# Keys stacked by DMA and the second attention taken batch by batch, in a two-layer decoder kernel

## The reference, cut to what matters

```python
# experts of layer 0: each token sums its 4 experts' rows, then a layer norm -> x
routed = zeros_like(x).at[tok].add(out_slots * flat_w[order][:, None])
# attention of layer 1, masked
q = einsum('bsh,he->bse', x, w_q)          # 16 heads x 128
k, v = split(einsum('bsh,he->bse', x, w_kv), 2)   # 4 groups x 128 each
probs = softmax(q @ k.T * 128 ** -0.5); ctx = probs @ v; out = ctx @ w_dense
# recurrence: query x, keys and values the context
log_D = ...; D = exp(log_D - max_log_D)     # 128 x 384 causal cells per head
qk = einsum('bhsd,bhtd->bhst', qh, kh) / sqrt(dh)
C = qk * D; h = (C / normalizer) @ vh; out = layernorm_per_head(h)
```

## Time and profile before

| | us |
|---|---|
| median of 3 runs | 1097.9 (1096.1 to 1100.84) |
| profiled execution, its own time | 1096.5 |
| its span, first to last instruction | 1094.5 |
| TensorE busy in it | 999.0 (91%) |
| VectorE, ScalarE, GpSimd busy | 717.9, 608.3, 459.8 |
| mean granted TensorE clock | 0.958 |

### The profile page before, as it was taken

The page is one execution under the profiler, slowest core; times in us unless marked ns, Lnnn a source line. Parts: engine busy times, 40 slices in busy tenths (PEclk is TensorE's granted clock), DMA queues, the critical chain, the costliest instruction groups (busy, mean ns, idle before and its releaser), DMA issues. The chain is left out here.

```text
span 1094.5 us, 18969 instructions
## 1 busy us (share of the span) xinstructions
PE 999.0 (91%) x6064; PEld 815.0 (74%) x6064; DVE 717.9 (66%) x2146; ACT 608.3 (56%) x1654; POOL 459.8 (42%) x473
## 2 busy tenths in 40 slices
PE   7999999998996799669899999988878889999996
PEld 5998899887883689537678888965445568777775
DVE  5666766663588456446655767646787557888886
ACT  3656565656222455336576776547874556555553
POOL 5787667761287344366111110210137214444321
PEclk9999999999998899869899999989998989999998
DMA  6732111000011799624301101001003011112101
GB/s 207 257 124 79 30 31 29 16 15 2 1 63 52 253 345 338 212 73 140 95 20 60 33 25 40 1 22 52 2 2 116 1 58 58 58 58 67 50 1 39
DMA packets 83784, 85.61 MB, mean 78 GB/s; under 512 B 8577, under 2 KB 75975, under 8 KB 83568
## 3 DMA queue, kind: packets, MB, share of 16 engines
q1 hardware_dynamic: 79776, 75.59, 21.4%
q0 software_dynamic: 3072, 7.34, 2.2%
q10 hardware_dynamic: 848, 1.57, 0.4%
HBM read 63.36 MB, written 22.02 MB: 78 GB/s over the span
## 5 line engine op out<-in xcount | busy, mean ns | idle before, releaser
L579 POOL TENSOR_TENSOR a_qk<-h,a_by_sin 128x512 f32<-128x512 f32 x64 | 81.9, 1280 | 5.0
L352 DVE CUSTOM_DVE_ANT_0 h<-a_score_ps,mask_bf 128x128 f32<-128x128 f32 (+1 forms) x128 | 40.7, 355 | 64.5 <-PE a_score_ps L345 64.3
L1286 POOL TENSOR_TENSOR a_w_l<-a_w,a_w_h 128x256 fp32r<-128x256 f32 x30 | 21.8, 728 | 115.6 <-ACT a_w_h L1479 115.4
L358 ACT ACTIVATE y_moe<-y_moe,a_nmax 128x128 f32<-128x128 f32 x64 | 25.6, 400 | 75.9 <-DVE a_nmax L352 75.9
L339 DVE COPY a_probsT<-a_turn_ps 128x384 f32<-128x384 f32 x64 | 34.9, 546 | 48.2 <-PE a_turn_ps L269 48.2
L1025 POOL TENSOR_TENSOR e_w_l<-e_w,e_w_h 128x512 fp32r<-128x512 f32 x32 | 40.8, 1276 | 53.1 <-ACT e_w_h L1093 53.1
L80 PE MATMUL a_proj_ps<-a_x_l,a_w_h 128*128 128x512 f32 x128 | 57.2, 447 | 3.6 <-POOL a_w_l L584 3.4
L459 PEld LDWEIGHTS a_proj_ps<-a_w,xT 128*128 128x128 f32 x512 | 59.6, 192 | 0.9 <-issue 0.2
L459 PE MATMUL a_proj_ps<-a_w,xT 128*128 128x128 f32 x512 | 59.8, 275 | 0.0
L755 PE MATMUL t_y_ps<-wo,attnT 128*128 128x256 f32 x256 | 58.7, 383 | 0.0
L2629 POOL TENSOR_TENSOR m_up_l<-m_up_w,m_up_h 128x1024 fp32r<-128x1024 f32 x8 | 19.5, 2434 | 90.1 <-ACT m_up_h L2601 90.1
(11 more groups left out here) (464 smaller groups left out, 3516.2 us busy)
## 6 DMA issues: line engine op xcount, KB each, us to landing
slots<-zeros SPq DMA_DIRECT2D x4, 2048.0 KB, 8.0
e_rows<-slots SPq DMA_DIRECT2D x32, 256.0 KB, 4.7
e_w<-in_L_ffn_w_dram SPq DMA_DIRECT2D x32, 256.0 KB, 4.9
out_slots<-e_out SPq DMA_DIRECT2D x32, 256.0 KB, 4.2
e_w<-in_L_ffn_w_dram SPq DMA_DIRECT2D x32, 128.0 KB, 4.3
a_w<-in_L_attn_w_q_dram SPq DMA_DIRECT2D x32, 128.0 KB, 2.2
m_up_w<-in_up_dram SPq DMA_DIRECT2D x8, 512.0 KB, 3.7
a_w<-in_L_attn_Wq_dram SPq DMA_DIRECT2D x16, 128.0 KB, 2.3
```

The lines of the kernel that those rows point to most:

```text
L352: done = dve.tensor_tensor_reduce(self.probs[:, b, cells], self.score_ps[:, r, cells], self.k.mask_bf[:, cells], -1.0, 3e38, ALU.add, ALU. ...
L358: act.activation(self.probs[:, b, 0:P], self.probs[:, b, 0:P], ACT.Exp, bias=self.nmax[:, b, 0:1], scale=-1.0, accum_out=self.total[:, b, ...
L579: pool.tensor_tensor(qk[:, par, 0 if what == "q" else 1, half * HALF:(half + 1) * HALF], by_cos[:, r, :], by_sin[:, r2, :], ALU.add).then_ ...
```

## The change

Second attention: units go batch by batch, over all heads of a batch. A step now makes two heads' queries for one batch (256 tokens), from a weight tile of 128x512, with 12 matmuls of 256 columns; there are still 32 steps. Keys are made per batch and group. Keys and values are kept for two batches, and `q` and the weight tiles get places of their own. Each gather has its own semaphore, and VectorE adds a row as soon as it has landed. Two tiles are prepared per batch, during the batch before.

Keys of the recurrence: SyncE stores the context's two parts to DRAM during the projection (4 stores of 512 KB) and loads them back in stacked form, 8 loads of 256 KB for each half, the first half during the projection, the second at the start of the recurrence. The `spread` constant is halved. The gates block then makes only the 16 stacks of x.

Around it: the block with two loads is gone; the twelve small loads are issued half by SyncE, half by GpSimd, and TensorE waits per batch instead of SyncE for all; two of the mixture's loads move into the recurrence; `C` gets its own memory.

```diff
-    STEPS = 2 * H
+    PAIRS = H // 2
+    STEPS = B * PAIRS
...
-                 ("x", 2)]
...
+        first = [("x", 0), ("v", 0), ("x", 1), ("v", 1), ("k", (0, 0)), ("q", 0), ("k", (1, 0))]
...
+            step = u // 2
+            return step, 2 * (step % PAIRS) + u % 2, step // PAIRS
...
+                gather(0)
+                gather(1)
+                ln.power(pool, 0)
+                ln.power(pool, 1)
+                gather(2)
+                for b in range(1, B):
+                    step, t = PAIRS * (b - 1), QT * b
+                    cut_low(step + 2)
+                    if b == 1:
+                        gather(t + 1, early)
+                    cut_low(step + 3)
+                    ln.power(pool, t)
+                    if b == 1:
+                        gather(t + 1, late)
+                    cut_low(step + 4)
...
+                        for a in range(2):
+                            for c in range(DC):
+                                last = product(pe, out[:, a * S:(a + 1) * S], weights(which, c, a),
+                                               x_p[:, c, b * S:(b + 1) * S], c == 0, c == DC - 1)
...
-                    dve.wait_ge(fetched[t], TOP0 * 16)
                     for j in range(TOP0 - 1):
+                        dve.wait_ge(fetched[t][j], 16)
...
+            @block.sync            # projection
+            def _(sp):
+                for c in range(DC):
+                    for part, (done, rows) in enumerate(((c_high, k.c_p.h), (c_low, k.c_p.l))):
+                        sp.wait_ge(done, c + 1)
+                        sp.dma_start(k.key_parts[part * D + c * P:part * D + (c + 1) * P, :], rows[:, c, :].bitcast(F32)
+                                     ).then_inc(k.keys_stored, 16)
+                sp.wait_ge(projected, 1)
+                sp.wait_ge(wo_low, WO_CUTS)
+                sp.wait_ge(k.keys_stored, 16 * 2 * DC)
+                load_keys(sp, k, 0)
...
+def load_keys(sp, k, half):
+    for part in range(2):
+        source = k.key_parts[part * D:(part + 1) * D, half * HALF:(half + 1) * HALF].rearrange("(c i w) t -> i w c t", i=2, w=LW)
+        for i in range(2):
+            for again in range(2):
+                first = i * 4 * LW + part * 2 * LW + again * LW
+                sp.dma_start(k.keys[half][first:first + LW, :, :].bitcast(F32), source[i]).then_inc(k.keys_in[half], 16)
...
-                for n in range(4 * STACKS):
+                for n in range(2 * STACKS):                       # stacks in the gates block
...
+            @block.gpsimd          # gates
+                pool.wait_ge(nM_done, 1)
+                spread_rows(pool, 1)
+                spread_rows(pool, 3)
...
-                sp.wait_ge(k.nM_in, 16 * B * 3)
+                spread_rows(sp, 0)
+                spread_rows(sp, 2)
...
+                    if h == 0:                                     # recurrence
+                        pe.wait_ge(k.nM_in[b], 16 * 3)
...
-        layer1_lstm_load(nc, k, I)
```

More of the change, by code:

```diff
@@ L1247, in of, with keys, value @@
         def of(u):
[L1249 to L1256, removed]
+            step = u // 2
+            return step, 2 * (step % PAIRS) + u % 2, step // PAIRS
+        def keys(b, i, j):
+            return slice(b % KEPT * S + i, b % KEPT * S + j)
+        def value(t):
+            return t % (KEPT * QT)
         with nc.Block() as block:
@@ L1290, in _ @@
                 ln.power(pool, 0)
+                ln.power(pool, 1)
                 gather(2)
[L1292 to L1312, removed]
+                for b in range(1, B):
+                    step, t = PAIRS * (b - 1), QT * b
+                    early, late = (0, 1), (2, 3)
+                    cut_low(step + 2)
[6 more added lines that the diff above has]
+                    cut_low(step + 4)
+                    cut_low(step + 5)
+                    ln.power(pool, t + 1)
+                    cut_low(step + 6)
+                    if b + 1 < B:
+                        gather(t + 2, early)
+                    cut_low(step + 7)
+                    if b + 1 < B:
+                        gather(t + 2, late)
+                    cut_low(step + 8)
+                    if b + 1 < B:
+                        gather(t + 3, early)
+                    cut_low(step + 9)
+                    if b + 1 < B:
+                        gather(t + 3, late)
+                for step in range(STEPS - PAIRS + 2, STEPS):
                     cut_low(step)
@@ L1363, in mix @@
                     g = head // HPG
-                    at.mix(pe, u, u % 4, lambda j: v[:, 2 * b + j, g * HD:(g + 1) * HD])
+                    at.mix(pe, u, u % 4, lambda j: v[:, value(QT * b + j), g * HD:(g + 1) * HD])
                 for one in first:
@@ L1487, in _ @@
                 keep("v", 0)
-                keep("x", 1)
-                keep("v", 1)
-                ln.squares(act, 2)
-                for one in first[-4:]:
+                for one in first[2:]:
                     keep(*one)
-                ln.squares(act, 3)
+                cut_high(2)
                 for u in range(UNITS):
@@ L1675, in layer1_gates @@
         nM, left, left2 = (m.sb(f"g_{n}", [P, CAUSAL]) for n in ("nM", "left", "left2"))
-        parts = m.sb("g_parts", [P, 3, CAUSAL], BF16)
+        parts = k.nM_parts
         x_p = Parts(m, "g_x", [P, DC, T])
         st_ps = m.ps("g_st_ps", [P, 4, 512])
-        BY_DVE = [n for n in range(4 * STACKS) if n >= 12 and n % 2]
-        BY_ACT = [n for n in range(4 * STACKS) if n not in BY_DVE]
+        BY_DVE = [11, 13, 15]
+        BY_ACT = [n for n in range(2 * STACKS) if n not in BY_DVE]
         x_high, x_low = m.sem("g_x_high"), m.sem("g_x_low")
@@ L1798, in _, with spread_rows @@
                 dve.wait_ge(kept, 1)
+            def spread_rows(queue, b):
+                for i in range(3):
+                    queue.dma_start(k.nM_rows[i * ROWS:i * ROWS + LH, b, :], parts[b * ROWS:b * ROWS + LH, i, :]
+                                    ).then_inc(k.nM_in[b], 16)
             @block.gpsimd
```

194 lines of the change are left out of this document (88 added, 106 removed).

## The result

| | before | after |
|---|---|---|
| median, us | 1097.12 (1096.1 to 1100.84, 4 runs) | 1086.26 (1081.75 to 1087.43, 4 runs) |
| ratio, 95% interval | | 0.9889 (0.9862 to 0.9916) |
| profiled execution; its span | 1096.5; 1094.5 | 1087.43; 1085.1 |
| mean granted clock | 0.958 | 0.960 |

The change takes 1.1% off by the ratio, 10.9 us by the medians. So most of this part asks which terms were too small, and whether errors hide each other. They do.

A forecast was written before the change was run, and what follows sets the result against it. TensorE, busy 91% of the span, was taken as the bound. Terms: -5.1 - 1.0 - 1.1 - 1.5 + 1.4 + 0.4 = -6.9 us, from the median 1097.9 to 1091.0 us; range 1082 to 1098.

The forecast's parts named there:

- Gates block: Gates block without key stacks: ends at 745.4, held by GpSimd's six loads at 1.1 us each; gain 5.1 us.
- The lower bound: Gates block: GpSimd's six small loads at SyncE's 0.63 us each end at 742.5, behind VectorE; gain 7.5 us.
- The block with two loads: Between projection and gates: one border and two issues go; gain 1.0 us.
- The keys: Recurrence's keys by DMA: loads land by 731, by the 256 KB row (4.7 us), needed at about 746; zero cost.
- The serial bound: Key loads, the other end: eight one after the other at 4.7 us each take 37.6 us, landing at 752.
- The start: Attention's start: tile 1 is normed 2.0 us earlier, first scores at 485.5 instead of 486.0; gain 1.1 us.
- The first twelve units: Attention's first twelve units: stalls sum to 5.0 us against 6.5, half clock stays; gain 1.5 us.
- The rival with a chance of 0.20: Attention: the stall at the 3 MB goes wholly, giving back 3.2 us and 3 us of half clock; 1084.8; chance 0.20.
- the 17 us: Attention's first units: step 7's weights land 17 us after the cut on which step 6's load hangs; before, 17.8.
- The rest of the attention: Later attention: narrower query steps lose 1.4 us, batch borders 0.4 us; ScalarE's longer cuts, 0.23 us a step, hidden.
- The slower rival, the ring of two weight tiles: Attention: landings of 256 KB tiles over 7.3 us decide the step; at 9.5 us about 1124; chance 0.05.
- The rival in which the gates block's wait changes owner: Gates block: GpSimd's plain loads take 2 us each, or keys land near 752; 5.1 us go; 1096.1; chance 0.22.

The follow-up runs named there:

- rows_by_sync: The changed kernel with all twelve small loads into the recurrence's rows issued by SyncE, none by GpSimd; 1089.5 us, ratio 0.9933.
- block_back: The changed kernel with the small block of its own for the two loads put back ahead of the gates; 1089.6 us, ratio 0.9937.
- keys_later: The changed kernel with the eight loads of the first keys issued at the start of the gates block, not during the projection; 1094.7 us, ratio 0.9987.
- cut_early_spread: `after_spread` with, from unit 14 on, ScalarE's high cut of a weight tile behind its unit's copies and one step earlier; 1083.8 us, ratio 0.9865.
- keys_only: The changed kernel with the second attention and the gathers' semaphores left as in the kernel before; 1087.8 us, ratio 0.992.
- one_wait: The changed kernel with VectorE waiting for all four gathers of a tile ahead of its first addition; 1086.9 us, ratio 0.9919.
- after_spread: The changed kernel with the 3 MB of later loads spread over steps from step 8 on, not in one block behind step 6; 1084.9 us, ratio 0.988.

## Why the prediction was right, and where its terms were wrong

The ranking of the stages was right: the gates block is most of it. The time fell by 10.9 us between the medians, against 6.9 forecast.

*Gates block.* Forecast -5.1, measured -7.0. VectorE's end was forecast as 16.5 us after the gates' first operation (743.0) and came at 16.9. The step that failed is the price of GpSimd's plain load: 1.1 us, taken from its indirect ones, measured 0.51. The lower bound, SyncE's 0.63, was nearer, and gave 7.5. That GpSimd would hold the block came true by 0.06 us only, and through the landing of its last load, which the working left out, not through its issues; `rows_by_sync` shows that the split is worth 3.0 us, as the working gave for the lower bound (3.3).

*The block with two loads.* Forecast -1.0, measured -1.3, and 1.3 to 1.5 by `block_back`.

*The keys.* Zero cost was right, by a reason that was wrong. Eight loads don't land after 4.7 us each, side by side; they land one after another, 2.2 us apart, and take 19.9 us. They had over 31 us. The serial bound was too long, the chosen row too short, and `keys_later` shows that with 13.5 us less cover the change is worth nothing: the small loads behind them come late first.

*The start.* Forecast -1.1, for tile 1. Tile 1 is normed 15.05 us after the first gather for 17.13, 2.1 us earlier (forecast 2.0). First scores come 1.8 us earlier in this pair, 1.5 in the mean of eight traces (23.6) against five (25.1). The working missed that the larger weight tiles would delay the fourth gather, and also that the separate waits pay for it.

*The first twelve units.* Forecast -1.5 with the half clock staying. `cut_low(4)` ended 7.88 us after the scores of unit 4 (forecast 7.6), and the query step waited 0.93 and a `mix` before it 0.84 (forecast 1.85 together). But step 7's weights landed 15.1 us after step 6's issue (503.26 to 518.40), not 17, and TensorE lost 0.81 us, not 3.2, under full clock. The rival with a chance of 0.20 is what happened: 4.5 of the stall's 5.6 us are gone. The step that failed is the 17 us, which took SyncE's issues and the landing to stay as they were: the eleven issues took 8.4 us for 9.6, and step 7's weights landed 6.4 us after their issue for 7.8. The rest of the chain was as told. With this stall two of the prediction's own signs of being right (3 us with half clock behind; GpSimd's sixth issue as the last thing in the gates block) didn't show, and one of its signs of being wrong, a stall that is gone, did.

*The rest of the attention.* Forecast +1.4 for the narrower steps, +0.4 for borders, and ScalarE's longer cuts "hidden". Measured: +1.3 for the narrow steps (0.043 each), and 2.5 for the cuts where they stand, by `cut_early_spread`. The argument for "hidden" was that ScalarE is busy 71%. That is a mean over 100 us; in units 20 and 21, and again in 36 and 37, its queue has no gap ahead of the copy for which TensorE waits. This is the failed step on the side of loss: the waits stand in the middle of a batch, where the next batch's keys and tiles are prepared, and not at the three borders, where the trace shows none. With the stall's 5.6, of which 1.1 stay, the stretch balances within the noise: -5.6 + 1.1 + 2.5 + 1.3 = -0.7, measured -1.4 in this pair and -0.9 between the means (186.2 and 185.3).

So two errors with opposite signs, 3 us too little for the stall and 2.0 too little for what is lost behind it, left the attention near the sum forecast for it (-1.5 + 1.4 + 0.4 = +0.3, measured -0.9 to -1.4), and the gates block's load price made the largest single part of the difference (1.9 us of 4.6 in the table's four rows). That the attention's sum came out near its forecast is luck.

The slower rival, the ring of two weight tiles, didn't come: ScalarE waited for a tile twice, 2.6 us in all. The rival in which the gates block's wait changes owner didn't come either, though `keys_later` is its case, by other transfers than the ones named.

## What to carry to other kernels

A block of large loads for later stages in the queue that also feeds a ring of two tiles cost a stall here and then TensorE's half clock; spreading the block over the steps gave 5.6 us with some fifteen lines of code, more than the rewritten attention. When a cut or copy on ScalarE gets longer or jobs move beside it, count its queue from the last thing it waited for to the copy that the bound engine waits for, in the fullest unit, not its busy share. And compare stretches between the same two instructions, in several traces, before believing 3 us of a whole time.

## What the runs showed of the hardware

The recurrence runs the same work in all fourteen traces, and took 70.9 to 75.9 us from its first operation to the router's first, in step with the granted clock: 0.98 gives 70.9, 0.95 gives 71.7 to 71.9, 0.91 gives 73.8 to 74.2, 0.87 gives 75.6 to 75.9, with the keys' loads beside it or without. Two of these stretches, of `keys_only` and of `one_wait`:

```profile
742.20:817.76 75.56, 63.76 (x681) 34.55 (x681) 53.84 (x126) 57.13 (x173) 15.55 (x13) 0.87 0.27 35
```

```profile
741.08:812.78 71.70, 59.51 (x681) 32.24 (x681) 53.67 (x126) 56.63 (x173) 15.52 (x12) 0.95 0.28 37
```

This alone moves the whole time by up to 5 us, as much as the parts of the change that were to be told apart.

A plain load issued by GpSimd takes 0.49 us of that engine (median), one by SyncE 0.59, both of 12 KB; GpSimd's indirect ones take 0.95.

Eight loads of 256 KB into 16 partitions each, issued within 4 us, land one after another, some 2.2 us apart. Loads of 12 KB behind them and behind 1.3 MB of others land after 8 to 11.5 us for 1.7 (`keys_later`): what is in flight, not their size, is their price.

GpSimd's part of a block ends 0.3 us after its last load has landed (nine traces); SyncE's doesn't wait for its landings (`rows_by_sync`). So in `after_spread`, where GpSimd's last load took 2.3 us to land instead of 1.6, the gates block ended 1.1 us after VectorE was done.
